# Gate and up products inside attention's steps, down and output projection in one last stage

## The reference

```python
xn = _layernorm(x)
s = attention(xn, wq, wk, wv, wo)          # 32 heads of 32, 8 key/value heads, rotary, causal softmax
w_gu = sc_gu[g] * (nibble_gu - (zero_gu[g] + 1))     # 1024 x 5504, 4-bit weights, groups of 128
gate, up = xn @ w_gu[:, :2752], xn @ w_gu[:, 2752:]
h = silu(gate) * up
w_d = sc_d[g] * (nibble_d - (zero_d[g] + 1))         # 2752 x 1024
out = x + s * silu(h @ w_d)
```

## Time and profile before

| | |
|---|---|
| median of 3 runs | 2513.79 us (2512.66 to 2514.32) |
| profiled execution | 2516.59 us, its span 2514.5 us |
| mean granted clock of PE | 0.973 |
| PE busy | 2377.0 us, 95% of the span |
| DVE, ACT, POOL busy | 1545.8, 748.2, 942.3 us |
| bytes read from and written to HBM | 88.76 MB, 47.42 MB |

### The profile page before, as it was taken

How to read it: one execution, slowest core, us unless ns; L and a number is a source line. 1 busy time by engine, 2 the same in 40 slices (tenths; PEclk the granted TensorE clock), 3 DMA queues, 4 the chain that set the end, 5 groups by cost and what they waited for, 6 DMA issues and landing times.

```text
span 2514.5 us, 46178 instructions
## 1 busy us (share of the span) xinstructions
PE 2377.0 (95%) x17048; PEld 1229.9 (49%) x17048; DVE 1545.8 (61%) x2800; ACT 748.2 (30%) x1469; POOL 942.3 (37%) x619
## 2 busy tenths in 40 slices
PE   6999889999999699989999999999999999999998
PEld 3555356666666444434444444444444444444432
DVE  4655488888888577355555555646454555556465
ACT  3222157777777532211111111010101010202022
POOL 2555469999999600021121212121212120202035
PEclk9999979999999899999999999999999999999998
DMA  5332312221222264200000000000000000000056
GB/s 159 97 84 64 86 43 72 72 71 59 70 72 72 89 198 163 82 16 13 12 13 13 12 12 12 5 19 3 21 0 24 0 24 0 24 0 19 0 172 234
DMA packets 129662, 138.26 MB, mean 55 GB/s; under 512 B 33106, under 2 KB 106421, under 8 KB 129148
## 3 DMA queue, kind: packets, MB, share of 16 engines
q1 hardware_dynamic: 127228, 127.96, 16.8%
q10 hardware_dynamic: 2304, 8.39, 0.8%
HBM read 88.76 MB, written 47.42 MB: 54 GB/s over the span
## 4 chain that ended last, share of the span: by engine, by line
PE 53%; DVE 3%; issue 1%; ACT 0%; POOL 0%; DVEq 0%; POOLq 0%
PE dn_ps L1474 18%; PE gate_ps L1455 17%; PE up_ps L1455 16%; PE s_ps L1424 1%; DVE zero L1542 1%; DVE wf L1554 0%; DVE dif L1548 0%; PE s_ps L1432 0%; ACT arena L1636 0%; PE z_ps L1424 0%; DVE acc L1586 0%; DVE nib L1523 0%; DVE zhalf L1537 0%; DVE idf L1502 0%; DVE acc L1579 0%
## 5 line engine op out<-in xcount | busy, mean ns | idle before, releaser
L1455 PE MATMUL gate_ps<-xT,wg 128*128 128x512 f16 x2112 | 789.1, 381 | 3.8 <-POOL wg L1676 3.8
L1455 PE MATMUL up_ps<-xT,wg 128*128 128x512 f16 x2016 | 766.1, 380 | 0.0
L577 POOL TENSOR_TENSOR p_lo<-probs 128x1152 f16<-128x1152 f32 (+1 forms) x256 | 501.2, 1994 | 48.8 <-ACT probs L741 48.7
L1474 PE MATMUL dn_ps<-wd,hT 128*128 128x512 f16 (+1 forms) x2112 | 471.9, 383 | 3.1 <-DVE acc L1579 3.1
L1676 POOL TENSOR_TENSOR wg<-wf,wg 128x512 f16<-128x512 f32 (+1 forms) x88 | 99.8, 1134 | 869.9 <-ACT wg L1622 869.9
L741 ACT ACTIVATE probs<-sc_ps 128x512 f32<-128x512 f32 (+3 forms) x768 | 351.0, 490 | 123.7 <-PE sc_ps L685 105.1
L1474 PEld LDWEIGHTS dn_ps<-wd,hT 128*128 128x128 f16 (+1 forms) x2112 | 202.2, 98 | 270.2 <-issue 31.5
L1579 DVE TENSOR_TENSOR acc<-acc,dn_ps 128x512 f32<-128x512 f32 x320 | 219.8, 687 | 184.7 <-PE dn_ps L1474 184.5
L1455 PEld LDWEIGHTS gate_ps<-xT,wg 128*128 128x128 f16 x2112 | 208.5, 99 | 242.0 <-issue 9.8
L790 DVE TENSOR_REDUCE shift<-mx_wide_ps 128x1 f16<-128x1024 f32 (+3 forms) x256 | 262.0, 1023 | 84.6 <-PE mx_wide_ps L667 84.5
L1455 PEld LDWEIGHTS up_ps<-xT,wg 128*128 128x128 f16 x2016 | 197.6, 98 | 229.9 <-issue 2.4
(11 more groups left out here) (130 smaller groups left out, 2973.7 us busy)
## 6 DMA issues: line engine op xcount, KB each, us to landing
o_scratch<-o SPq DMA_DIRECT2D x16, 1040.0 KB, 4.9
a<-o_scratch SPq DMA_DIRECT2D x16, 1040.0 KB, 5.4
arena<-q_scratch SPq DMA_DIRECT2D x48, 256.0 KB, 3.4
arena<-in_qw_d SPq DMA_DIRECT2D x42, 256.0 KB
xin<-in_x SPq DMA_DIRECT2D x16, 512.0 KB, 3.7
s_scratch<-arena ACTq DMA_DIRECT2D x16, 512.0 KB, 2.6
xT<-in_x SPq DMA_DIRECT2D x32, 256.0 KB, 4.8
xT<-s_scratch SPq DMA_DIRECT2D x32, 256.0 KB, 5.6
```

Of the source, the lines that this page charges most:

```text
L577: eng.tensor_tensor(p_lo[:, r % 2, c], probs[:, r % 2, c], p_hi[:, r % 2, c], ALU.subtract).then_inc(done, 1)
L1455: last = pe.matmul(to[q][:, :], wg[:, u, wp, s, g * P:(g + 1) * P], xT[:, xp, s, t * BANK:(t + 1) * BANK], start=(s == 0 and k == 0), stop ...
L1474: last = pe.matmul(dn_ps[n][:, :], hT[0:w, hp, e, tokens], wd[0:w, wp, e, n * BANK:(n + 1) * BANK], start=(e == 0 and p == 0), stop=(e == ...
```

## The change

What is done in the four stages is arranged anew, in three.

- `project_qkv` also makes the tables (`piece`, `select`), in pieces on DVE between its own work. Zeros are kept as whole 4-bit values, so the rebuilding needs fewer steps on DVE.
- `attend_and_expand` runs 88 units of gate and up (22 tiles x 4 chunks of 512 tokens), one in each step. 64 of the steps also have a head; four steps lead in, before the first, and 24 follow without a head. In each slot six products of gate (slots 0 to 3) or up (slots 4 to 7) come first. Weights are rebuilt in half rounds of 256 columns: gate and up in slots 1 and 5 of each step, down in slots 3 and 7 of the last two steps of a tile. Hidden values and rebuilt down weights go to HBM.
- The maxima use the high parts alone, 32 rows, of two heads: one product on rows 0 to 31, one on rows 32 to 63, into two banks (`mx_ps[:, e]`), which are one buffer: the next piece waits until DVE has reduced both. DVE, not PE, turns the shifts. POOL makes all low parts of the probabilities. There are two score banks instead of three.
- `finish` takes 16 tiles of 128 tokens: down (22 tiles of hidden features summed in PSUM, not by DVE), output projection, and the final Silu, product and sum. Hidden values, attended sums and x are loaded for each tile, the down weights once.

The core of the diff (of the changed kernel's `attend_and_expand`; the old functions of the same names are in the listing above):

```diff
+    SC_BANKS = 2
+    LEAD = 6
+    MAXIMA = [(7, 0), (7, 1), (0, 0), (6, 0), (6, 1), (1, 0), (5, 0), (2, 0), (5, 1), (4, 0), (3, 0), (4, 1)]
+    LOW = [ORDER[n:n + 2] for n in range(0, ST, 2)]
...
+        sc_ps = [ctx.enter_context(nc.psum_tensor(f"sc_ps{i}", [P, BANK], F32)) for i in range(SC_BANKS)]
+        mx_ps = ctx.enter_context(nc.psum_tensor("mx_ps", [P, 2, BANK], F32))
+        o_ps = ctx.enter_context(nc.psum_tensor("o_ps", [P, BANK], F32))
+        gate_ps = ctx.enter_context(nc.psum_tensor("gate_ps", [P, BANK], F32))
+        up_ps = ctx.enter_context(nc.psum_tensor("up_ps", [P, BANK], F32))
+        sz_ps = ctx.enter_context(nc.psum_tensor("sz_ps", [P, 2, HALF], F32))
...
+                for e in range(2):
+                    rows = slice(e * HD, (e + 1) * HD)
+                    last = pe.matmul(mx_ps[:, e, 0:end - first], qT[rows, u, q + e, t * P:(t + 1) * P],
+                                     kT[rows, u, first:end], start=True, stop=not diagonal)
+                if diagonal:
+                    for e in range(2):
+                        last = pe.matmul(mx_ps[:, e, t * P - first:end - first], identb[:, :], maskb[:, :],
+                                         start=False, stop=True)
+                last.then_inc(mx_ready, 1)
...
+                    rows = sel_gu[:, :].rearrange("g (p s) -> g s p", s=KT)[:, n, :]
+                    pe.matmul(sz_ps[:, 0, 0:2 * w], rows, st[:, u, :, 0:w], start=True, stop=True)
+                    last = pe.matmul(sz_ps[:, 1, 0:2 * w], rows[0:G_GU, :], zt[:, u, :, 0:w], start=True, stop=True)
...
+                if to is None:
+                    return
+                cols = slice(0, P) if i < ST // 2 else slice(P, 2 * P)
+                for s in range(2 * (i % (ST // 2)), 2 * (i % (ST // 2)) + 2):
+                    for k, (wp, xp) in enumerate([(0, 0), (0, 1), (1, 0)]):
+                        last = pe.matmul(to[:, :], wg[:, u, wp, s, cols], xT[:, xp, s, tokens],
+                                         start=(s == 0 and k == 0), stop=(s == KT - 1 and k == 2))
...
+            def step(m, r):
+                for i in range(ST):
+                    gate_up(m, r, i)
+                    scores(m, r, i)
+                    for slot, kind, n, j, u, number, _ in halves(m, r):
+                        if slot == i:
+                            rebuild(kind, n, j, u, number)
+                    if maxima_at(m, r, i):
+                        maxima(*maxima_at(m, r, i))
+                    if i == 1:
+                        outputs(*at(m, r, -1, R), 0)
+                    if i >= 1:
+                        outputs(*at(m, r, -1, R), i)
...
+            def step(m, r):
+                for i in range(ST):
+                    exps(m, r, i)
+                    if i == 0:
+                        copy_sums(*at(m, r, -2, R))
+                    if i == 1:
+                        highs(*at(m, r, -1, R), 7)
+                    if i == 2:
+                        rounded(*at(m, r, -1, R))
+                    if i in (3, 5, 7):
+                        highs(m, r, i - 2)
+                    if i == 5:
+                        gated(m, r)
+                wo_high(m, r)
...
+            def step(m, r):
+                for i in range(ST):
+                    if i == 0:
+                        gated(*at(m, r, -1, R))
+                    if maxima_at(m, r, i):
+                        maxima(*maxima_at(m, r, i))
+                    for slot, kind, n, j, u, number, p in halves(m, r):
+                        if slot == i:
+                            rebuild(kind, n, j, u, number, p)
+                    if i == 2:
+                        select(m, r)
+                wo_low(m, r)
...
+            def step(m, r):
+                low(m, r, 0)
+                lows(*at(m, r, -1, R), 7)
+                hidden(*at(m, r, -1, R))
+                low(m, r, 1)
+                lows(m, r, 1)
+                low(m, r, 2)
+                lows(m, r, 3)
+                low(m, r, 3)
+                lows(m, r, 5)
```

and of `finish` on PE:

```diff
+            def down(u, half, j):
+
+                wt = tile_width(j)
+                src = wd_of(j)[1]
+                for k, (hp, wp) in enumerate([(0, 0), (0, 1), (1, 0)]):
+                    last = pe.matmul(dn_ps[u][:, half, :], hT[0:wt, u, hp, j, :],
+                                     src[0:wt, wp, half * BANK:(half + 1) * BANK],
+                                     start=(j == 0 and k == 0), stop=(j == FTILES - 1 and k == 2))
+                if j == FTILES - 1:
+                    last.then_inc(dn_ready, 1)
+
+            def tile(m, u):
+                n = number(m, u)
+                pe.wait_ge(ht_loaded[u], 32 * (m + 1))
+                for half in range(2):
+                    pe.wait_ge(g_done, 2 * (n - 2) + half + 1)
+                    for j in range(FTILES):
+                        down(u, half, j)
+
+            turn(0, 0)
+            project(0, 0)
+            turn(0, 1)
+            project(0, 1)
+            turn(1, 0)
+            for u in range(2):
+                pe.wait_ge(ht_loaded[u], 32)
+            for j in range(FTILES):
+                pe.wait_ge(wd_loaded[wd_of(j)[0]], 16)
+                for u in range(2):
+                    for half in range(2):
+                        down(u, half, j)
+            project(1, 0)
+            turn(1, 1)
+            project(1, 1)
...
+            def body(m):
+                for u in range(2):
+                    turn(m + 1, u)
+                    tile(m, u)
+                    project(m + 1, u)
```

More of the change, by code:

```diff
@@ new lines, in unpack, with values @@
+            def unpack(words, g, to):
+                n = words.shape[1]
+                whole = tb_zn[0:g, 0:n * NIB].rearrange("g (c k) -> g c k", k=NIB)
+                def values():
+                    for k in range(NIB):
+                        last = dve.tensor_scalar(whole[:, :, k], words, 4 * k, 15,
+                                                 ALU.logical_shift_right, ALU.bitwise_and)
+                    return last
+                return [values, lambda: dve.tensor_copy(to, tb_zn[0:g, 0:n * NIB])]
@@ L588, in steps, with count @@
                     step(m, r)
-            for r in range(R + 3):
-                step(*at(NH // R - 1, 0, r, R))
+            for k in range((NH // R - 1) * R, NU + 2):
+                step(*at(0, 0, k, R))
+        def count(m, r):
+            return R * m + r
         @block.sync
@@ new lines, in finish, with wd_of, number, exists @@
+        wd_loaded = [sem(f"wd_loaded{i}") for i in range(len(groups))]
+        x_v = x.rearrange("b (t p) d -> (b t) p d", p=P)
+        out_v = out.rearrange("b (t p) d -> (b t) p d", p=P)
+        def wd_of(j):
+            for i, (to, at_tile, first, n) in enumerate(groups):
+                if first <= j < first + n:
+                    return i, to[:, :, at_tile + j - first, :]
+        def number(m, u):
+            return 2 * m + u
+        def exists(m, u):
+            return inside(m, u, TT)
@@ L1010, in _, with body @@
             turned(1, 0)
-            post(0, 0)
-            post(0, 1)
-            with act.Fori(1, TT // 2 - 1) as m:
-                step(m, 0)
-                step(m, 1)
-            step(TT // 2 - 1, 0)
-            step(TT // 2 - 1, 1)
+            for u in range(2):
+                for half in range(2):
+                    gate(0, u, half)
+            take(1, 0)
+            turned(1, 1)
+            take(1, 1)
+            high(2, 0)
+            high(2, 1)
+            def body(m):
+                for u in range(2):
+                    turned(m + 1, u)
+                    gate(m, u, 0)
+                    gate(m, u, 1)
+                    take(m + 1, u)
+                    high(m + 2, u)
@@ L1134, in _ @@
+            normalise(0, 0)
+            low(0, 0)
+            normalise(0, 1)
+            low(0, 1)
+            turned(0, 0)
+            normalise(1, 0)
+            low(1, 0)
+            turned(0, 1)
+            normalise(1, 1)
+            low(1, 1)
+            turned(1, 0)
+            for u in range(2):
+                for half in range(2):
+                    weigh(0, u, half)
+            turned(1, 1)
             for u in range(2):
-                normalise(1, u)
-                low(1, u)
@@ L1137, in _, with body @@
-            turned(1, 0)
-            with dve.Fori(1, PIECES // 2 + 1) as m:
+                normalise(2, u)
+                low(2, u)
+            def body(m):
                 for u in range(2):
-                    step(m, u)
-                    piece(m - 1, u)
-            for m in range(PIECES // 2 + 1, TT // 2):
-                step(m, 0)
-                if m == TT // 2 - 2:
-                    select()
-                step(m, 1)
-                if m == TT // 2 - 2:
-                    down_tables()
```

1508 lines of the change are left out of this document (690 added, 818 removed).

## The result

The changed kernel takes 2620.28 us, the median of 4 runs (2618.03 to 2622.09), against 2513.82 of the kernel before on the same chip: a ratio of 1.0424, 95% interval 1.0406 to 1.0442. It is 4.2% slower. The forecast was 2537, and the range ended at 2615. The sign was right; the size was not: 0.9% slower was forecast.

What follows compares the result with a forecast made beforehand. PE was taken to bound the kernel, except attention, led by POOL. Terms 318 + 42 + 1235 + 15 + 261 + 14 + 653 = 2538 us gave a 2537 us median, 0.9% slower, range 2470 to 2615.

Steps and rivals of the forecast that it cites:

- First stage, 318: Up to the first maxima: PE's products cover DVE's added table work; 318 us, range 314 to 328, against 316.4 before.
- Lead-in, 42: Four steps before the first gate product: 20 maxima pieces, PE and DVE taking turns on one buffer; 42 us, range 26 to 46.
- Pair at once, 1.42 a step: Maxima in each step: two heads' products on different rows and banks run together; 1.42 us, against 2.4 in turn.
- Pauses, 1.7 a step: PE in each step: 16 changes to or from products on 32, 8 or 21 rows, 0.106 us each; 1.7 us, uncovered.
- ACT's wait, 0.5 a step: PE waits for a score bank in slot 7, behind ACT's Silu and table loads; 0.5 us, range 0 to 1.5.
- The drain of 1.38 us: ACT's table switches: a drain beside each 1.28 us load; rival with the step 2.8 us longer, 2714 us, chance 0.02.
- Step, 19.43: Each of 64 steps with a head and a gate-up unit takes 19.43 us; 1235 us in all after 9 off.
- Returns, 15: Five returns of the loop over heads: PE's earlier standstill less some cover from longer products, 3 us each, 15 us.
- Units without a head and the change of stage: 24 gate-up units after the heads take 261 us; the passage to the last stage's first transpose takes 14 us.
- Last stage, 653: Down and output projection: 643 us of PE work, 4 of slow clock, 6 for the last half; 653 us.
- the rivals: Maxima products in turn 0.15, no pause on 32 rows 0.13, better covers 0.15, a queue running behind 0.13, drain 0.02.
- the signs that the prediction gave for being wrong: A pause under 0.085 or over 0.13 us, pair products in turn, or a step's wait for DVE or ACT over 1 us.

Runs made afterwards that it cites:

- e8: Changed kernel with POOL's subtraction for the low part of x done on 16 of 1024 columns (that computation left out): 2596.1 us, ratio 1.0336.
- e5: Changed kernel with the gate and up tables worked out once on 128 rows and the heads' loads put back where they were: 2563.5 us, ratio 1.0207.
- e10: Changed kernel with tables on 128 rows, maxima on 96 rows, zeros on 72 and 85, head loop written out, and two maxima buffers in the lead-in: 2479.7 us.
- e3: Changed kernel with the zeros of the rebuilding on 72 rows (85 for down), the added rows zero: 2585.2 us, ratio 1.0288.
- e6: Changed kernel with maxima products on all 96 rows and zeros on 72 and 85 rows: 2568.6 us, ratio 1.0229.
- e4: Changed kernel with the loop over the heads written out, so no engine jumps back: 2593.5 us, ratio 1.0321.
- e13: The kernel before the change, with only its loop over the heads written out: 2492.5 us, ratio 0.9925.

## Why the prediction missed

*First stage, 318.* This step failed: "DVE made them among 125.3 us of work there; even all of that beside its 168.8 here is under 316, so PE's products cover them." Two errors are in the sentence. It compares sums over the whole stage, while the pieces stand in the middle half, where DVE's 68 us became 153.5 against PE's 122 (the windows above). DVE leads there, and PE waits. And it carries durations from a stage in which POOL stands still into one in which it is busy for 45% (e8: 524 ns free, 1,958 beside POOL). e5 puts the size at some 49 us. "3 us now and then" was 26.6 and 12.4 us of waits and a clock that fell with them. The prediction also passed over that the heads' loads move behind the last pieces, in SP's queue between the last units and their stores (5.8 us). In e5 11 us are left over 318. By the sum that was made for after, its projections end at 310.7, 8.5 us later than before (PE lost 5.5 in the window of the pieces for down), the first half rounds take 2.2 and the wait is 1.7 longer, 12.4 in all, of which the forecast had allowed 1.6.

*Lead-in, 42.* Right (37.5), for the reason given: a single buffer in turns; e10 takes it away and gains 13.2.

*Pair at once, 1.42 a step.* Right, shown by the half-clock rows above.

*Pauses, 1.7 a step.* Right: 0.10 a change in the slots shown, and e3 and e6 take them away. That eight or 32 rows change the shape and 72, 85, 96, 97 don't is now shown in both directions. The Trainium skill, TensorEngine Tiling (Array Packing), Key Properties, says that a change of mode drains TensorE and that tiles on rows of their own run in parallel. This case's rows agree with both halves, and put 0.10 us on the drain.

*ACT's wait, 0.5 a step.* 15.6 us in all, 0.25 a step; inside its bounds. The rest was covered by the pauses, which give ACT time: take the pauses away (e6) and it comes to 0.53. The drain of 1.38 us that the prediction quoted from the Trainium skill, ScalarE: Activation LUTs, isn't there in after either: on ACT's timeline a load starts 0.01 us behind Silu, and the exp 0.01 behind the load.

```profile
1090.31 0.60 ACT L1142 ACTIVATE h<-gate_ps 128x512 f32<-128x512 f32 x1
1090.92 1.28 ACT L1101 ACT_TABLE_LOAD   x1
1092.21 0.88 ACT L1101 ACTIVATE room<-sc_ps 128x512 f32<-128x512 f32 x2
```

*Step, 19.43.* Four steps without a return go from 754.62 to 831.55, 19.23 each. Right. The 64 of e4 take 1228.3 us for the 1235 of the sum.

*Returns, 15.* This term was mis-sized: e4 shows 27. The term counted the standstill of the earlier trace rows and took something off for longer products; e13 shows that even before a return cost 4.1 us and not 2.8, the rest presumably slow clock behind it. The line of the steps and their returns came out right in part by luck: the steps were 7 too high and the returns 12 too low.

*Units without a head and the change of stage.* 262.9 for 261, 13.6 for 14.

*Last stage, 653.* 13.6 too low. Its first products wait for DVE and ACT, and in its first 39 us the DMA engines are fully busy with loads. PE's waits of after behind 1940 (beside the one wait that is the change of stage), and the windows:

```profile
PE tro_ps L1480 <- ACT ah L1552: 13.6, 2, 11.6
PE out_ps L1495 <- DVE aT L1643: 7.9, 2, 4.8
```

```profile
1960.00:1975.00 15.00, 13.05 (x64) 5.99 (x64) 3.30 (x5) 2.33 (x3) 0.00 (x0) 0.87 1.04 399
1975.00:1992.00 17.00, 15.37 (x76) 7.19 (x77) 5.29 (x6) 3.49 (x4) 0.00 (x0) 0.90 1.04 399
```

2.0 + 7.9 us of waits are two tiles that turn one after the other with nothing between (the 11.6 is the change of stage). The other 3.7 us aren't taken apart; the clock is low in this stretch (0.50 in the 15 us ahead, 0.87 and 0.90 here), and for that the forecast had counted 4 us. The loads moved 399 GB/s, and no wait for them shows: the fear of 148 GB/s was unfounded.

None of the rivals named the first stage, and none of the signs that the prediction gave for being wrong came: the change of shape cost 0.10, the pair ran at once, and the waits for DVE and ACT in a step were far under 1 us. It failed where it had named no sign. What the forecast had in its sum made the change 23 us slower; the cover in the first stage, which was assumed and never cut by stretches, cost 66 more. Of the other 16, the last stage (13.6) and the returns (12) are set against a shorter lead-in and shorter steps.

## What to carry to other kernels

Before you hide work beside an engine that "has room", cut the stage where the work will stand, not where the stage begins and ends, and add it to what the engine does in that stretch. Take the length of a DVE operation only from a stretch in which POOL does what it will do beside it; if a short operation hardly gets shorter with a fortieth of the columns and ends with one of POOL's, it is being held. Lay small tables over all 128 rows before you cut them into pieces: 64 operations on 8 rows took 16.2 us here. And count the changes of shape on PE: a pair of small products at once gains nothing up to some 500 columns if both neighbours have another shape.

## What the hardware showed that was not expected

- The tables' DVE operations from SBUF to SBUF waited for POOL's running operation: 16 columns took up to 2.11 us beside a POOL operation of 2.65 us and ended 0.03 behind it, and 688 columns took 0.52 us with POOL's made short.
- A reciprocal of 128 x 512 on DVE took 3.35 us, 6.5 ns a column, while a reciprocal of one column takes 0.16.
- A return of the loop over eight heads cost 4.1 us before and 5.4 us after the change (20.4 and 26.8 over five), of which 2.8 and 3.4 stood as waits of PE; the changed kernel written out shows no such wait, though PE has some 1,370 products in every eight steps (10,991 in 64).
- Two products on 32 rows each, into two banks, run at once: some 0.43 us for a pair of 512 columns at clock 0.50 (0.53 with the change of shape behind it), and 0.86 for two on 96 rows.
- 16 DMA engines moved 399 GB/s over 32 us from 1960 us on.
